# Rotation from ScalarE's copy, cosines in a PSUM scratch bank, score differences in the probabilities' buffer, and another slot order

## The reference

```
x = x + 0.5 * stack(layernorm(x))
x = x + attention_block(layernorm(x))
x = x + 0.5 * stack(layernorm(x))

stack, 6 times:
  q, k, v = split(shift_tokens(x) @ Wqkv)           # 16 heads of 64
  q, k = l2norm(q) * qs, l2norm(k) * ks             # then rotary, with scale and 1/scale
  q = q*cos*scale + rotate_half(q)*sin*scale
  k = k*cos/scale + rotate_half(k)*sin/scale
  x = softmax(mask(q k^T * 8), windows of 32 looking one back) v @ Wo + x
  a, gate = split(layernorm(shift_tokens(x)) @ W1 + b1)
  x = a * gelu(gate) @ W2 + b2 + x
```

## Time and profile before

| | |
|---|---|
| median of 3 runs | 3613.35 us (3610.72 to 3627.78) |
| profiled execution | 3621.26 us, its span 3619.1 us |
| busy: PE, DVE, ACT, POOL | 3322.5, 2800.4, 2482.6, 2720.1 us |
| mean granted TensorE clock | 0.969 of full speed |

### The profile page before, as it was taken

How to read it: one execution, slowest core, us unless ns; L and a number is a source line. 1 busy time by engine, 2 the same in 40 slices (tenths; PEclk the granted TensorE clock), 3 DMA queues, 4 the chain that set the end, 5 groups by cost and what they waited for, 6 DMA issues and landing times. The chain is left out here.

```text
span 3619.1 us, 152088 instructions
## 1 busy us (share of the span) xinstructions
PE 3322.5 (92%) x64040; PEld 2535.6 (70%) x64040; DVE 2800.4 (77%) x4983; ACT 2482.6 (69%) x3080; POOL 2720.1 (75%) x2152
## 2 busy tenths in 40 slices
PE   6899999999999999998677899999999999999996
PEld 4777777777777777776335777777777777777774
DVE  5778878788878878876447788778888878878883
ACT  4677777777767777775225677777777777777773
POOL 5888888788878878875007888888888888888881
PEclk8999999999999999999889999999999999999998
DMA  3333333333333333332002333333333333333320
GB/s 96 77 83 82 80 83 82 78 86 79 79 84 78 80 87 77 81 88 64 6 0 67 79 85 82 80 84 78 83 86 78 81 83 80 81 83 77 78 74 25
DMA packets 208997, 272.66 MB, mean 75 GB/s; under 512 B 55748, under 2 KB 103744, under 8 KB 208320
## 3 DMA queue, kind: packets, MB, share of 16 engines
q1 hardware_dynamic: 208320, 262.94, 28.2%
HBM read 60.35 MB, written 1.05 MB: 17 GB/s over the span
## 5 line engine op out<-in xcount | busy, mean ns | idle before, releaser
L1240 POOL TENSOR_TENSOR V<-RAWQK,TAB 128x512 f32<-128x512 f32 x768 | 953.2, 1275 | 443.5 <-PE PS L340 434.3
L388 PE MATMUL PS<-WH,XH 128*128 128x512 f32 x1152 | 518.4, 450 | 99.9 <-ACT VS L770 86.3
L770 ACT ACTIVATE VS<-PS 128x1024 f32<-128x1024 f32 x192 | 196.5, 1023 | 481.0 <-PE PS L390 357.2
L1282 POOL TENSOR_TENSOR V<-V,U 128x1024 f32<-128x1024 f32 x192 | 455.6, 2373 | 14.9
L390 PE MATMUL PS<-WL,XH 128*128 128x512 f32 x1152 | 465.5, 404 | 0.0
L389 PE MATMUL PS<-WH,XL 128*128 128x512 f32 x1152 | 464.5, 403 | 0.0
L1266 POOL TENSOR_TENSOR V<-V,U 128x1024 f32<-128x1024 f32 x192 | 457.5, 2383 | 0.0
L1275 POOL TENSOR_TENSOR V<-V,RN 128x1024 f32<-128x1024 f32 x192 | 372.2, 1938 | 93.7 <-DVE RN L918 92.1
L340 PEld LDWEIGHTS PS<-EYE,V 128*128 128x128 f32 x3072 | 348.2, 141 | 110.2 <-issue 99.0
L510 PEld LDWEIGHTS PS<-OT,WO 128*128 128x128 f32 x3072 | 373.6, 192 | 21.4 <-issue 5.1
L340 PE MATMUL PS<-EYE,V 128*128 128x128 f32 x3072 | 371.3, 274 | 10.3 <-ACT OT L777 5.1
(11 more groups left out here) (162 smaller groups left out, 7100.0 us busy)
## 6 DMA issues: line engine op xcount, KB each, us to landing
V<-VS SPq DMA_DIRECT2D x3072, 64.0 KB
ROTB<-c_rot SPq DMA_DIRECT2D x192, 128.0 KB, 2.5
WSTAGE<-wqkv SPq DMA_DIRECT2D x33, 512.0 KB
WO<-wo SPq DMA_DIRECT2D x12, 512.0 KB, 3.8
W<-w SPq DMA_DIRECT2D x12, 341.0 KB, 3.1
QKS<-qks SPq DMA_DIRECT2D x12, 128.0 KB, 3.7
W<-w SPq DMA_DIRECT2D x12, 114.0 KB
RAWQK<-x SPq DMA_DIRECT2D x4, 256.0 KB, 3.7
```

The source lines that it names most:

```text
L388: pe.matmul(o, XH[:, p, :], WH[:, w, cols], start=True, stop=False)
L1240: ins = pool.tensor_tensor(paired(V[:, k])[:, :, :, h * half:(h + 1) * half], split(RAWQK[:, k])[:, :, :, (1 - h) * half:(2 - h) * half], ...
L1282: pool.tensor_tensor(V[:, 1], V[:, 1], U[:, 1], ALU.add).then_inc(k_turned, 1)
```

## The change

- VectorE multiplies RAWQK, ScalarE's copy, by the cosines instead of the PSUM rows; the cosines are first copied from TAB into the scratch bank (COS in B_NORM), one copy of 128 x 64 for queries and one for keys, each followed by a drain. So the banks of the raw queries and keys are free after ScalarE's copy.
- The difference of scores and maximum goes to PR instead of back to the score banks, and the exponential works in place in PR. The score banks are free after the difference, which now waits until the last PR has been transposed.
- All steps have other banks and another order in the slots, and several work one chunk later or earlier than before. The feed-forward part is one slot later everywhere.
- The loads of the weights: the thirds of Wqkv behind chunks 1, 8 and 12, W1 behind 9, W2 and the attention's small tensors behind 11.
- The norms of the stacks' inputs use banks 4 and 5 instead of 0 and 2.

```diff
-B_Q = 3
-B_K = 5
-B_V = 5
-B_TQ = 3
+B_Q = 2
+B_K = 0
+B_V = 2
+B_TQ = 0
 B_TK = 0
-B_S = 3
-B_O = 5
+B_S = 4
+B_O = 2
 B_P = 0
-B_TO = 0
-B_WO = 2
-B_F1 = 2
-B_F2 = 1
-B_F3 = 0
-LAG, SEED_LAG, CHAIN_OFF, CHAINS = 7, 0, 2, 108
+B_TO = 2
+B_WO = 1
+B_F1 = 6
+B_F2 = 4
+B_F3 = 5
+LAG, SEED_LAG, CHAIN_OFF, CHAINS = 7, 0, 3, 109
+WQKV_AT, W1_AT, W2_AT, ATTN_AT = (1, 8, 12), 9, 11, 11
...
+        COS = PS[:, B_NORM, 0:2 * DH].rearrange("p (k d) -> p k d", k=2)
...
-                    after(use(exp_done, c - 2), use(exp_done, c - 2), use(q_kept, c - 2), use(uq_done, c - 1))
+                    after(use(o_scaled, c - 4), use(o_scaled, c - 4), use(v_kept, c - 2), use(o_kept, c - 5), use(q_copied, c - 1))
                     project(0, c, B_Q).then_inc(q_raw, 1)
...
                 def ffn_third(n):
                     q, g = phase(n)
                     if not (q != 1 and 0 <= g < NGR):
                         return
-                    after(use(k_kept, n + 1), use(o_kept, n - 1), use(p_kept, n), third(n - 1), third(n - 2), third(n - 3))
+                    after(use(shifted, n + 1), use(shifted, n + 1), third(n - 1), third(n - 2), third(n - 3))
...
-                for t in range(108):
+                for t in range(109):
+                    queries(t)
+                    keys(t)
                     scores_a(t - 2)
+                    turn_outputs(t - 4)
                     scores_b(t - 2)
+                    turn_weights(t - 3)
+                    ffn_first(t - 3)
                     values(t - 1)
+                    turn_queries(t - 1)
+                    ffn_third(t - 3)
+                    ffn_second(t - 3)
+                    turn_keys(t - 1)
+                    weigh_a(t - 3)
+                    weigh_b(t - 3)
                     project_out(t - 4)
-                    keys(t)
-                    turn_weights(t - 2)
-                    queries(t)
-                    turn_outputs(t - 3)
-                    weigh_a(t - 2)
-                    ffn_first(t - 2)
-                    turn_keys(t - 1)
-                    turn_queries(t - 1)
-                    weigh_b(t - 2)
-                    ffn_second(t - 2)
-                    ffn_third(t - 2)
...
                         return
                     act.wait_ge(shifted, count(inv, c))
-                    held(p_rows, count(inv, c - 1))
-                    held(sum_done, count(inv, c - 1))
-                    if inv == 0 and c == 0:
-                        act.wait_ge(w_split, 3)
-                    act.activation(PR[:, :, :].rearrange("p (j r) k -> p r j k", r=2),
-                                   rows(B_S).rearrange("p r (j k) -> p r j k", k=2 * WIN), ACT.Exp).then_inc(exp_done, 1)
+                    act.activation(PR[:, :, :], PR[:, :, :], ACT.Exp).then_inc(exp_done, 1)
...
                     dve.wait_ge(tab_done, count(inv, c))
+                    dve.tensor_copy(COS[:, 0, :], TAB[:, c % 2, 0:DH])
+                    dve.drain()
                     dve.wait_ge(q_copied, count(inv, c))
                     held(q_turned, count(inv, c - 1))
-                    dve.tensor_tensor(paired(U[:, 0]), rows(B_Q).rearrange("p r (j d) -> p r j d", d=DH),
-                                      per_dim(TAB[:, c % 2, 0:DH], DH), ALU.mult).then_inc(uq_done, 1)
+                    dve.tensor_tensor(paired(U[:, 0]), split(RAWQK[:, 0]), per_dim(COS[:, 0, :], DH),
+                                      ALU.mult).then_inc(uq_done, 1)
...
                     s = rows(B_S).rearrange("p b (j k) -> p b j k", k=2 * WIN)
                     dve.tensor_reduce(MX[:, :, :], s, AX.X, ALU.max)
                     dve.drain()
-                    dve.tensor_tensor(s, s, rep(MX[:, :, :], [P, 2, NP_, 2 * WIN], 3), ALU.subtract).then_inc(shifted, 1)
+                    held(p_rows, count(inv, c - 1))
+                    if inv == 0 and c == 0:
+                        dve.wait_ge(w_split, 3)
+                    dve.tensor_tensor(PR[:, :, :].rearrange("p (j r) k -> p r j k", r=2), s,
+                                      rep(MX[:, :, :], [P, 2, NP_, 2 * WIN], 3), ALU.subtract).then_inc(shifted, 1)
...
                 for t in range(111):
+                    cos_keys(t - 1)
+                    ffn(t - 4)
+                    sum_keys(t - 1)
+                    scale_outputs(t - 4)
+                    sum_queries(t - 1)
+                    add_back(t - 5)
+                    norm(t - 1)
+                    cos_queries(t)
                     row_sum(t - 3)
-                    sum_keys(t - 1)
-                    scale_outputs(t - 3)
-                    ffn(t - 3)
-                    sum_queries(t - 1)
                     row_max(t - 2)
-                    norm(t - 1)
-                    add_back(t - 4)
-                    cos_keys(t)
                     scale_keys(t - 1)
-                    cos_queries(t)
...
-                for t in range(109):
-                    sin_queries(t - 2)
-                    low_part(t - 1)
-                    add_keys(t - 2)
-                    add_queries(t - 2)
-                    ffn(t - 3)
+                for t in range(110):
+                    ffn(t - 4)
                     scale_queries(t - 2)
                     table(t)
+                    sin_queries(t - 1)
+                    add_queries(t - 1)
+                    low_part(t)
                     sin_keys(t - 1)
+                    add_keys(t - 1)
 
...
-                    if i in (1, 5, 9) and w + 1 < 2 * DEPTH:
-                        k = i // 4
+                    if i in WQKV_AT and w + 1 < 2 * DEPTH:
+                        k = WQKV_AT.index(i)
...
-                    if i == 11 and w + 1 < 2 * DEPTH:
+                    if i == ATTN_AT and w + 1 < 2 * DEPTH:
...
-                    if c >= CH and i == LAG:
+                    if c >= CH and i == W1_AT:
...
                         load_w1(w)
-                    if c >= CH and i == LAG + 2:
+                    if c >= CH and i == W2_AT:
```

More of the change, by code:

```diff
@@ L430, in turn_keys @@
                     pe.wait_ge(k_scaled, count(inv, c))
-                    after(use(o_kept, c - 2), use(p_kept, c - 1), third(c - 2), use(k_kept, c - 1), third(c - 3), third(c - 4))
-                    after(use(o_kept, c - 2), use(p_kept, c - 1), second(c - 2), use(k_kept, c - 1), second(c - 3), second(c - 4))
+                    after(use(q_kept, c), use(p_kept, c - 2), use(k_copied, c + 1), use(k_kept, c - 1))
+                    after(use(q_kept, c), use(p_kept, c - 2), use(k_copied, c + 1), use(xb_done, c - 4), use(k_kept, c - 1))
                     turn(lambda h: V[:, 1, 2 * h:2 * h + 2, :].rearrange("p r d -> p (r d)"), B_TK).then_inc(k_rows, 1)
@@ L447, in scores_a @@
                         return
-                    after(use(q_kept, c), use(uq_done, c + 1), use(exp_done, c - 1), use(exp_done, c - 1))
+                    after(second(c - 2), use(shifted, c - 1), use(shifted, c - 1), second(c - 3), second(c - 4))
+                    after(third(c - 2), use(shifted, c - 1), use(shifted, c - 1), third(c - 3), third(c - 4))
                     for r in range(2):
@@ L482, in weigh_a @@
                         return
[L483 removed]
+                    after(use(v_kept, c + 2), use(o_kept, c - 1), use(q_copied, c + 3), use(o_scaled, c - 1), use(o_scaled, c - 1))
                     pe.wait_ge(p_kept, count(inv, c))
@@ L496, in turn_outputs @@
                     pe.wait_ge(o_scaled, count(inv, c))
-                    after(use(p_kept, c + 1), third(c), use(k_kept, c + 1), use(o_kept, c - 1), third(c - 1), third(c - 2))
-                    after(use(p_kept, c + 1), second(c), use(k_kept, c + 1), use(o_kept, c - 1), second(c - 1), second(c - 2))
+                    after(use(q_copied, c + 4), use(o_scaled, c), use(o_scaled, c), use(v_kept, c + 2), use(o_kept, c - 1))
                     turn(lambda h: ON[:, 2 * h:2 * h + 2, :].rearrange("p r d -> p (r d)"), B_TO).then_inc(o_rows, 1)
@@ L507, in project_out @@
                     pe.wait_ge(o_kept, count(inv, c))
-                    after(first(c + 1), use(xb_done, c - 1), first(c + 0), first(c - 1))
+                    after(use(k_kept, c + 3), use(q_kept, c + 3), use(p_kept, c + 1), use(k_copied, c + 4), use(xb_done, c - 1))
                     for h in range(NP_):
@@ L524, in ffn_first @@
                         return
-                    after(use(xb_done, n - 2), first(n - 1), first(n - 2), first(n - 3))
+                    after(first(n - 1), first(n - 2), first(n - 3))
                     if q == 0:
@@ L539, in ffn_second @@
                     if q == 1 and 0 <= g - 1 < NGR:
-                        after(use(k_kept, n + 1), use(o_kept, n - 1), use(p_kept, n), second(n - 1), second(n - 2), second(n - 3))
+                        after(use(shifted, n + 1), use(shifted, n + 1), second(n - 1), second(n - 2), second(n - 3))
                         if (g - 1) % NG == 0:
```

50 lines of the change are left out of this document (28 added, 22 removed).

## The result

The changed kernel takes 3691.41 us (median; 3686.26 to 3701.97), the kernel before 3612.03 on the same chip (3607.09 to 3627.78). The ratio is 1.022, with a 95% interval of 1.019 to 1.025: slower by 79 us. The forecast was slower by 0.5%, 3630 us. The sign and the full range (3545 to 3705) were right; the value was 61 us short, and the measured time lies above the 3600 to 3675 that the prediction gave to its own walk.

A forecast was written before the change was run, and what follows sets the result against it. TensorE, busy 92% of 3619.1 us, was taken as the bound, with SyncE's weight-load stalls costing 120 us. The sum 3621 - 120 + 94 + 28 + 15 = 3638 became 3630 us for the median, range 3545 to 3705.

The forecast's parts named there:

- its own walk: The forecast's main case, summing its terms to 3630 us, with its own range of 3600 to 3675; chance 0.4.
- What bounds the kernel, and the weight loads: TensorE bounds; SyncE's weight loads wait for GpSimd's subtraction, and moving them gains 120 us, bounds 96 and 124.
- The third subtraction: At ten layer boundaries TensorE waits 6.9 us for GpSimd, plus 2.5 us of clock: plus 94 us.
- Copies, PR, banks: 384 cosine copies on VectorE, difference in PR, freed banks: no term of their own, bounds nothing and 108 us.
- The new order: Four slots take 67.1 us against 66.5, 0.15 us more per slot: plus 28 us, bounds minus 83 and plus 92.
- the XL loop: Queries, turn, GpSimd's sine product, sum and XL, next queries: no slot can be shorter than 16.4 us.
- Edges: Starts and ends of both stacks: 10 us for first intervals, 5 for deeper ends, plus 15 us.
- The third rival: VectorE binds through the difference and scaled outputs, 0.5 us per slot and 12 per boundary: 3720 us; chance 0.2.
- The first rival: Banks freed earlier let TensorE run at its own pace part of the time: 3551 us; chance 0.25.
- the second: Rival: the boundary wait is short and leaves the clock alone, as GpSimd is ahead: 3591 us; chance 0.1.
- the fourth: Rival: the loads hold SyncE at other chunks and half of the 120 us stays: 3690 us; chance 0.05.

The follow-up runs named there:

- e1: The kernel before with only the thirds of the weights loaded behind chunks 1, 8 and 12 instead of 1, 5 and 9: 3507.37 us, ratio 0.970.
- e2: The changed kernel with all weight thirds split four slots earlier, loaded behind chunks 1, 4 and 8: 3620.06 us, ratio 1.001.
- f3: The changed kernel with the cosines copied for the first chunk of a stack only: 3696.77 us, ratio 1.022.
- h1: e2 with 8 instead of 16 window DMAs per chunk from a stack's third chunk on: 3586.92 us, ratio 0.992.
- h4: e1 with both rewrites (rotation from RAWQK with cosine copies, difference in PR) in the old order and banks: 3517.80 us, ratio 0.974.

## Why the prediction was right in sign and 61 us short

The medians, step by step: before to e1 -107, e1 to e2 +113, e2 to after +71. Together +77; the two medians on one chip gave +79. The forecast's +17 on 3613 was -120, +43 and +94. The sign was no luck: without the loop that the forecast left out (33 us) the same steps still add up to some 44 us slower.

- **What bounds the kernel, and the weight loads.** Right. The stalls of SyncE were real and are gone; 107 of 120 us.
- **The third subtraction.** Right in place, number and cause: ten waits, 6.5 us each (65.4 in 10) for 6.9, and 2.0 us of clock (the mean of the ten) for 2.5. The intervals say 86 us for 94. The step's claim that there is no cover was wrong in part: without the boundary waits 18 us of other waits come up, so that removing them gave 71.
- **Copies, PR, banks.** Within the bounds: 10 us in the old order, nothing in the new one. But the walk had VectorE last in the fourth slot, with the copies in it, and f3 shows no such thing. The banks were not run by themselves.
- **The new order: the step that failed.** Its walk came out in the sum. Queries to turn is 9.24 us for 9.2 (1467.18 to 1476.42 in the timeline), and four slots without DMA waits take 67.2 us (medians of h1: 16.53, 16.66, 17.11 and 16.90) for 67.1 (16.4, 16.4, 17.5 and 16.8). That is closer than its parts: three slots are 0.1 to 0.3 us longer and one is 0.4 shorter. But "plus 28 us" had two faults. The slots before were taken from one stretch of 66.5 us; the medians of e1, whose order is the old one, are 16.01, 16.97, 16.09 and 16.95, which is 66.0. Against e1 the stacks of h1 are 51 us longer instead of 28 (1595.7 + 1597.3 against 1572.5 + 1569.6), against h4, which has the rewrites, 45 (1571.8 + 1575.8). By the waits, most of it is the XL loop: TensorE's matmuls wait for XL 55 us in 82 waits in h1 and 12 us in 5 in e1. The other fault is a loop left out. The step listed the loops through GpSimd and VectorE and none through SyncE, although the diff moves the weighing from chunk t - 2 to t - 3 and leaves the values at t - 1. V2 has two halves, so the DMAs of chunk t - 1 need the half that chunk t - 3 has been weighed from. Before, that was a slot ago; now it is the end of the same slot. SyncE's row changed from waits for the values (911 us in 191, in e1) to waits for the weighing (948 us in 188). The loop is worth 33 us (e2 to h1).

```profile
SPq L1373 <- ACT VS L770: 911.0, 191, 163.9
```

- **Edges.** Plus 15 was too little, and put in the wrong place: outside the stacks h1 has 25 us more than h4 (first copy at 54.5 for 43.1, the middle 250.1 for 237.0, the end 1 us more). The first copy of raw queries or keys comes as early as it did (38.2 for 38.1); the values' copy stands 11 us later behind it, in both stacks, and the ends of the stacks are no shorter for that. So each stack's pipeline is some 12 us longer, where the forecast had 5 for both. The 10 us given to the first intervals did not come: the first six of both stacks take 192.7 us in h1 and 192.8 in h4.

So of the 113 us between e1 and e2, 10 are the rewrites, 33 the DMA loop, 45 longer slots and 25 the edges; the first two are differences of medians, the others of profiled executions, so that the sum is good to a few us. The third rival, VectorE as the bound at 3720, came nearest to the time but not by its mechanism: leaving out the copies (f3) changed nothing, and in the changed kernel TensorE's matmuls wait for the difference 3 times (2.6 us) and for the scaled outputs 11 times (6.3 us). The first rival, TensorE at its own pace, is excluded by 83 waits for XL and slots of 16.5 us and more; the second by the measured 6.5 us and the clock; the fourth by SyncE, which no longer waits for WL.

## What to carry to other kernels

When a change moves a consumer one step later and leaves its producer, walk every buffer between them, the DMA queue's too: a buffer of two halves gives one step of slack, and the move had used it up. Where relieving one suspected loop gives little, relieve two together before dropping it: 20 and 11 us apart were 61 together. Take the slot of the kernel before from medians by position over all periods: one clean stretch was 0.5 us off in 66, which was 20 us in the sum.

## What the runs showed of the hardware

- An issue of a window DMA takes SyncE 0.59 us, 0.63 from start to start, but 292 of 3072 in the changed kernel take 1.0 to 2.5 us, one or two in most groups of sixteen. So a group lasts 10.0 to 12.8 us, 11.3 as a median.
- TensorE, idle for 5.9 us, came back at 0.50 of its clock for 4 us, as it did in the earlier trace rows after 5.6 us.
- Two SBUF operands on VectorE beside a busy GpSimd doubled VectorE's product in this kernel (2425 against 1221 ns) and lengthened GpSimd's by up to 30% (2521 against 1941 ns). Where GpSimd was idle, ten times in 192, the same product took 1224 to 1226 ns.
